# Layer norm with tokens on partitions by eight turns, masks in 64x32 blocks, rope tables renewed one by one

## The reference

```
for i in range(6):
    x = attn_layer(shift_tokens(x), Wqkv[i], q_scale[i], k_scale[i], Wo[i]) + x
    x = ffn_layer(shift_tokens(x), ln_g[i], ln_b[i], W1[i], b1[i], W2[i], b2[i]) + x

def ffn_layer(x, g, bln, W1, b1, W2, b2):
    mu = x.mean(-1, keepdims=True)
    var = ((x - mu) ** 2).mean(-1, keepdims=True)
    xn = (x - mu) / jnp.sqrt(var + 1e-05) * g + bln
    a, gate = jnp.split(xn @ W1 + b1, 2, -1)
    return a * gelu(gate) @ W2 + b2
```

## Time and profile before

| | |
|---|---|
| median of 3 runs | 3816.27 us (3815.24 to 3817.18) |
| the profiled execution | 3817.41 us |
| its span, first to last instruction | 3815.5 us |
| mean granted PE clock | 0.981 of full |
| instructions | 146379 |
| span up to the layers | some 675 us |
| the layers | some 3125 us for 384 slots |

### The profile page before, as it was taken

One profiled execution on the slowest core, in us unless ns is written; L12 is line 12 of the kernel. 1 busy time (PEld: TensorE's weight loads), 2 busy tenths in 40 slices (PEclk: granted clock), 3 DMA queues, 4 the chain that ended last, 5 costly groups with the idle time before them and its releaser, 6 DMA issues.

```text
span 3815.5 us, 146379 instructions
## 1 busy us (share of the span) xinstructions
PE 3549.1 (93%) x60112; PEld 2231.2 (58%) x60128; DVE 3112.5 (82%) x4377; ACT 2650.5 (69%) x4972; POOL 2420.8 (63%) x2197
## 2 busy tenths in 40 slices
PE   5667676899999999999999999999999999999997
PEld 2222222466666666666666666666666666666664
DVE  4899998888888888888878888878888788888884
ACT  3545454677777777777777777777777777777775
POOL 0356555776666666666666666666666666666661
PEclk9889899999999999999999999999999999999999
DMA  3000000010111111111111111111111111111101
GB/s 78 0 0 0 0 0 0 26 37 28 33 35 48 37 33 32 32 48 37 37 33 32 43 43 35 30 32 32 48 41 34 32 32 48 37 37 29 33 28 38
DMA packets 64418, 120.05 MB, mean 31 GB/s; under 512 B 18196, under 2 KB 35986, under 8 KB 63634
## 3 DMA queue, kind: packets, MB, share of 16 engines
q1 hardware_dynamic: 63762, 110.70, 10.0%
HBM read 20.50 MB, written 2.10 MB: 6 GB/s over the span
## 4 chain that ended last, share of the span: by engine, by line
PE 79%; issue 2%; DVE 2%; ACT 1%; POOL 0%; DMA 0%; ACTq 0%; POOLq 0%; DVEq 0%; SPq 0%
PE qk L1130 17%; PE trb L1002 10%; PE ob L1188 10%; PE vob L1196 8%; PE vob L1136 8%; PE sc L1164 7%; PE sc L1215 6%; PE ob L1002 4%; PE sc L1222 3%; PE sc L1158 2%; PE vob L1238 1%; PE vob L1250 1%; DVE arena L889 0%; DVE ssq L895 0%; DVE arena L890 0%
## 5 line engine op out<-in xcount | busy, mean ns | idle before, releaser
L507 POOL TENSOR_TENSOR arena<-arena,rnorm 128x512 f32<-128x512 f32 x768 | 785.2, 1044 | 930.0 <-ACT rnorm L626 929.5
L500 POOL TENSOR_TENSOR arena<-arena 128x512 f32<-128x512 f32 x768 | 962.8, 1275 | 35.9 <-DVE arena L890 35.9
L633 ACT ACTIVATE arena<-trb 128x512 f32<-128x512 f32 x768 | 462.6, 602 | 441.6 <-PE trb L1002 441.6
L1130 PE MATMUL qk<-wqkv,xs 128*128 128x512 f32 x1536 | 729.4, 597 | 16.3 <-issue 9.2
L889 DVE TENSOR_TENSOR arena<-qk,tab_q 128x512 f32<-128x512 f32 x384 | 263.3, 686 | 455.0 <-ACT arena L619 447.6
L483 POOL TENSOR_TENSOR arena<-arena 128x512 f32<-128x512 f32 x256 | 300.0, 1182 | 346.4 <-DVE arena L859 333.8
L1002 PE MATMUL trb<-ident,arena 128*128 128x128 f32 x3072 | 482.3, 280 | 9.8 <-ACT arena L633 7.3
L1130 PEld LDWEIGHTS qk<-wqkv,xs 128*128 128x128 f32 x1536 | 292.7, 191 | 309.1 <-issue 291.7
L895 DVE TENSOR_REDUCE ssq<-arena 128x16 f32<-128x1024 f32 x384 | 463.7, 1207 | 0.0
L619 ACT ACTIVATE arena<-qk 128x512 f32<-128x512 f32 x768 | 426.8, 588 | 45.0 <-PE qk L1130 28.1
L1002 PEld LDWEIGHTS trb<-ident,arena 128*128 128x128 f32 x3072 | 346.7, 141 | 140.1 <-issue 88.3
(11 more groups left out here) (139 smaller groups left out, 5879.6 us busy)
## 6 DMA issues: line engine op xcount, KB each, us to landing
arena<-arena SPq DMA_DIRECT2D x192, 384.0 KB, 3.2
arena<-arena SPq DMA_DIRECT2D x192, 64.0 KB, 3.0
wqkv<-in_L_ffn_Wqkv SPq DMA_DIRECT2D x18, 512.0 KB, 4.6
wo<-in_L_ffn_Wo SPq DMA_DIRECT2D x6, 512.0 KB, 4.0
arena<-in_L_attn_x SPq DMA_DIRECT2D x8, 256.0 KB, 2.9
out<-arena SPq DMA_DIRECT2D x8, 256.0 KB, 2.2
w<-in_L_ffn_W SPq DMA_DIRECT2D x6, 341.0 KB, 2.9
arena<-in_sel SPq DMA_DIRECT2D x1, 1024.0 KB, 5.0
```

Of the source, the lines that this page charges most:

```text
L500: nc.gpsimd.tensor_tensor(ts[c * 2 + j][:, heads], tu[:, 0, heads], tu[:, 1, heads], ALU.add).then_inc(summed[0], 1)
L507: nc.gpsimd.tensor_tensor(part, part, rnorm[j][:, 8 * h:8 * h + 8].unsqueeze(2).to_broadcast([P, 8, HEAD]), ALU.mult) \
L633: A((qT, kT)[j][u][:, 4 * h:4 * h + 4, at_col:at_col + P], TRB.rearrange("p (a t) -> p a t", a=4), ACT.Copy) \
L1130: MM(QK[:, 512 * h:512 * h + 512], lhsT=xs[u][:, c * P:(c + 1) * P], rhs=wqkv[:, col:col + 512], start=True, stop=True) \
```

## The change

The norm of a group takes another way. In slot 19 (`LAG_TOKENS`) PE turns `xs2` in four blocks of 128x128, so that tokens lie on partitions (`VOB`). DVE sums each token's 128 features along the free axis (four sums for each partition) and subtracts the mean (`centre`). In slot 20 (`LAG_SQUARES`) ACT squares, and DVE sums again at the slot's end. In slot 21 (`LAG_BACK`) ACT takes logarithm and exponential of four numbers for each partition, DVE multiplies behind its rope, PE turns the result back in four blocks into the second half of `SC`, behind the down product, and ACT applies gain and offset on the way to `xnT`. The scores of the next slot wait for that. `v_unit` of slot 19 waits for the subtraction (`n_xc`). The copy of the layer's parameters moves from slot 22 to slot 21 behind the addition of the last down product.

The mask of a step is written by eight products instead of two, each on a 64x32 tile, with a semaphore increment in PE's queue ahead of them. The constant is changed so that rows 64 to 127 repeat rows 0 to 63. The rope tables of the next layer are multiplied one in each slot, in the slot behind a table's last use.

The diff, without the declarations of the new semaphores and of four small buffers `nsum`, `nvar`, `nlog`, `nrstd` (128x4):

```diff
@@ -39,7 +39,7 @@
 LAG_SCORES, LAG_SUM, LAG_PTURN, LAG_VALUES, LAG_OUT, LAG_ADD = 6, 7, 8, 9, 10, 11
-LAG_STAGE, LAG_MEAN, LAG_VAR, LAG_NORMED = 17, 19, 21, 22
+LAG_STAGE, LAG_TOKENS, LAG_SQUARES, LAG_BACK = 17, 19, 20, 21
 LAG_UP, LAG_DOWN = (23, 25, 27), 29
...
@@ -681,6 +695,12 @@
                     squares(*unit)
+                at_ = group_at(l, k, LAG_BACK)
+                if at_:
+                    act_e.wait_ge(n_var[0], at_[1] + 1)
+                    A(nlog[:], nvar[:], ACT.Ln, scale=1.0 / DIM, bias=eps[:, 0:1]).then_inc(n_log[0], 1)
+                    act_e.wait_ge(n_log[0], at_[1] + 1)
+                    A(nrstd[:], nlog[:], ACT.Exp, scale=-0.5).then_inc(n_rstd[0], 1)
                 up0, up1 = group_at(l, k, LAG_UP[0]), group_at(l, k, LAG_UP[1])
...
@@ -692,17 +712,17 @@
                     turned(*at_, 0)
-                at_ = group_at(l, k, LAG_MEAN)
-                if at_:
-                    item(act_e, ln_xc, at_[1] + 2 * GROUPS)
-                    A(sq2[0], xc[0], ACT.Square).then_inc(ln_sq[0], 1)
-                at_ = group_at(l, k, LAG_VAR)
-                if at_:
-                    item(act_e, ln_var, at_[1] + 2 * GROUPS)
-                    item(act_e, ln_out, at_[1] + (2 * GROUPS - 1))
-                    A(rstd[0], bank[2][:], ACT.Ln, bias=eps[:, 0:1]).then_inc(ln_log[0], 1)
-                    item(act_e, ln_log, at_[1] + 2 * GROUPS)
-                    A(rstd[0], rstd[0], ACT.Exp, scale=-0.5).then_inc(ln_rstd[0], 1)
+                at_ = group_at(l, k, LAG_SQUARES)
+                if at_:
+                    act_e.wait_ge(n_xc[0], at_[1] + 1)
+                    A(sq2[0], xc[0], ACT.Square).then_inc(n_sq[0], 1)
+                at_ = group_at(l, k, LAG_BACK)
+                if at_:
+                    if at_[0] == 0:
+                        item(act_e, lpar_done, l + (k - LAG_BACK) // LAYER)
+                    item(act_e, n_back, at_[1])
+                    A(xnT[:, at_[0] * GROUP:at_[0] * GROUP + GROUP], SC[:, 512:1024], ACT.Identity, scale=lpar[:, 0:1], bias=lpar[:, 1:2]) \
+                        .then_inc(n_out[0], 1)
                 at_ = step_at(l, k, LAG_VALUES)
...
@@ -871,12 +891,10 @@
 
-            def layer_tables(l, layer):
-
-                for c in range(CHUNKS):
-                    for tab, base, sc in ((tab_q, base_q, scale_q), (tab_k, base_k, scale_k)):
-                        V.tensor_tensor(tab[:, c], base[:, c], sc[:, ds(layer, 1), :].to_broadcast([P, 2, HEAD]), ALU.mult) \
-                            .then_inc(tabs_done[0], 1)
+            def layer_table(layer, c, j):
+
+                tab, base, sc = (tab_q, tab_k)[j], (base_q, base_k)[j], (scale_q, scale_k)[j]
+                V.tensor_tensor(tab[:, c], base[:, c], sc[:, ds(layer, 1), :].to_broadcast([P, 2, HEAD]), ALU.mult).then_inc(tabs_done[0], 1)
 
...
@@ -931,6 +949,17 @@
 
+            def centre(group, n):
+
+                dve.wait_ge(n_turned[0], n + 1)
+                tokens = VOB[:, :].rearrange("p (c f) -> p c f", f=DIM)
+                V.tensor_reduce(nsum[:], tokens, op=ALU.add, axis=AX.X).then_inc(n_sum[0], 1)
+                slot(dve, n_back, n)
+                dve.wait_ge(n_sum[0], n + 1)
+                V.scalar_tensor_tensor(out=xc[0].rearrange("p (c f) -> p c f", f=DIM),
+                                       in0=nsum[:, :].unsqueeze(2).to_broadcast([P, GROUP // P, DIM]), scalar=-1.0 / DIM,
+                                       in1=tokens, op0=ALU.mult, op1=ALU.add).then_inc(n_xc[0], 1)
+
             def layer_slot(l, k):
...
@@ -939,21 +968,21 @@
                 unit = unit_at(l, k, 0)
-                if unit and k % LAYER == 0:
-                    layer = l + k // LAYER
-                    if k:
-                        item(dve, roped, unit[0] * 2 + -1)
-                    layer_tables(l, layer)
-                    item(dve, tabs_done, layer * (2 * CHUNKS) + (2 * CHUNKS - 1))
+                if unit and k % LAYER < UNITS:
+                    dve.wait_ge(tabs_done[0], (l + k // LAYER) * UNITS + k % LAYER + 1)
                 if unit:
                     rope(*unit)
+                at_ = group_at(l, k, LAG_BACK)
+                if at_:
+                    dve.wait_ge(n_rstd[0], at_[1] + 1)
+                    tokens = xc[0].rearrange("p (c f) -> p c f", f=DIM)
+                    V.tensor_tensor(tokens, tokens, nrstd[:, :].unsqueeze(2).to_broadcast([P, GROUP // P, DIM]), ALU.mult).then_inc(n_scaled[0], 1)
                 at_ = step_at(l, k, LAG_SCORES)
...
                     maxima(*at_)
-                at_ = group_at(l, k, LAG_MEAN)
-                if at_:
-                    item(dve, ln_mean, at_[1] + 2 * GROUPS)
-                    V.tensor_tensor(xc[0], xs2.rearrange("p s t -> p (s t)"), bank[2][:], ALU.subtract).then_inc(ln_xc[0], 1)
+                at_ = group_at(l, k, LAG_TOKENS)
+                if at_:
+                    centre(*at_)
                 at_ = group_at(l, k, LAG_UP[1])
...
@@ -964,22 +993,29 @@
                     add_y(*at_)
+                at_ = group_at(l, k, LAG_BACK)
+                if at_ and at_[0] == 0:
+                    layer = l + (k - LAG_BACK) // LAYER
+                    if group_at(l, k, LAG_DOWN):
+                        item(dve, x_next, layer * GROUPS + -1)
+                    V.tensor_copy(lpar[:], lpar_all[:, ds(layer, 1), :].rearrange("p o n -> p (o n)")).then_inc(lpar_done[0], 1)
+                    item(dve, lpar_done, layer)
                 if unit:
                     square_sums(*unit)
-                at_ = group_at(l, k, LAG_NORMED)
-                if at_:
-                    if at_[0] == 0:
-                        layer = l + (k - LAG_NORMED) // LAYER
-                        V.tensor_copy(lpar[:], lpar_all[:, ds(layer, 1), :].rearrange("p o n -> p (o n)")).then_inc(lpar_done[0], 1)
-                        item(dve, lpar_done, layer)
-                    item(dve, ln_rstd, at_[1] + 2 * GROUPS)
-                    V.scalar_tensor_tensor(out=xc[0], in0=xc[0], scalar=lpar[:, 0:1], in1=rstd[0], op0=ALU.mult, op1=ALU.mult) \
-                        .then_inc(ln_aff[0], 1)
-                    item(dve, ln_aff, at_[1])
-                    V.tensor_scalar(xnT[:, at_[0] * GROUP:at_[0] * GROUP + GROUP], xc[0], lpar[:, 1:2], None, ALU.add).then_inc(ln_out[0], 1)
+                ahead = unit_at(l, k, 1)
+                if ahead and not isinstance(l, int) and LAYER - UNITS <= (k - 1) % LAYER:
+                    item(dve, roped, ahead[0] * 2 + 1)
+                    layer_table(l + 1, ahead[3], ahead[4])
+                at_ = group_at(l, k, LAG_SQUARES)
+                if at_:
+                    dve.wait_ge(n_sq[0], at_[1] + 1)
+                    V.tensor_reduce(nvar[:], sq2[0].rearrange("p (c f) -> p c f", f=DIM), op=ALU.add, axis=AX.X).then_inc(n_var[0], 1)
 
...
             dve.wait_ge(cleared[0], 2)
+            for c in range(CHUNKS):
+                for j in range(2):
+                    layer_table(0, c, j)
             item(dve, ln_out, 2 * GROUPS - 1)
...
@@ -994,7 +1030,7 @@
         def _(pe):
-            give_credits(pe, [x_turned, y_step, mo_done, vproj_done, tr_done, s_done, pt_done, pv_done, wo_done, y_done, f_turned])
+            give_credits(pe, [x_turned, y_step, mo_done, vproj_done, tr_done, s_done, pt_done, pv_done, wo_done, y_done, n_back, f_turned])
             MM = nc.tensor.matmul
...
@@ -1141,7 +1177,7 @@
 
-            def scores(s, B, u, j, n, up0, up1, up2, down):
+            def scores(s, B, u, j, n, up0, up1, up2, down, back):
 
...
@@ -1154,9 +1190,14 @@
                     item(pe, x_next, down[1])
-                for h in range(2):
-                    MM(SC[:, 512 * h:512 * h + 512], lhsT=ident16[:], rhs=mask[:, :].unsqueeze(1).to_broadcast([P, STEP_PAIRS, 2 * SPAN]),
-                       start=True, stop=True)
+                if back:
+                    pe.wait_ge(n_out[0], back[1] + 1)
+                pe.sem_inc(s_open[0], 1)
+                for g in range(4):
+                    for h in range(2):
+                        d, pick = slice(64 * h, 64 * h + 64), 64 * h + (WINDOW if g else 0)
+                        MM(SC[32 * g:32 * g + 32, 512 * h:512 * h + 512], lhsT=ident16[d, pick:pick + WINDOW],
+                           rhs=mask[d, :].unsqueeze(1).to_broadcast([64, STEP_PAIRS, 2 * SPAN]), start=True, stop=True, skip_group_check=True)
                 for a in range(STEP_PAIRS):
...
@@ -1229,13 +1270,7 @@
                 out_before = step_at(l, k - 1, LAG_OUT)
-                mean = group_at(l, k, LAG_MEAN)
-                var = group_at(l, k, LAG_VAR)
-                if var:
-                    pe.wait_ge(ln_sq[0], var[1] + (1 + 2 * GROUPS))
-                    if out_before:
-                        item(pe, x_added, out_before[0])
-                    MM(VOB[:, :], lhsT=meanw[:], rhs=sq2[0], start=True, stop=True).then_inc(ln_var[0], 1)
```

(35 more changed lines are left out.)

18 lines of the change are left out of this document (16 added, 2 removed).

## The result

The changed kernel took 4060.35 us (median of 4 runs, 4051.55 to 4073.37) against 3816.72 for the kernel before on the same chip: ratio 1.0639, 95% interval 1.0615 to 1.0664, 244 us slower. The forecast was 3891 us in a range of 3850 to 3940. Its sign was right, its size was not: the loss was three times the one it named. The profiled execution of after took 4055.68 us, its span 4053.8.

What follows compares the result with a forecast made beforehand. TensorE (93% busy) bounds the kernel; later transposes (+2.13 us) less three mask gains of 0.18 cost 1.6 us a group, 74 over 46 groups, with the tail +75 on 3816.3: 3891 us, range 3850 to 3940.

Steps and rivals of the forecast that it cites:

- What bounds the kernel, and where it bites: PE bounds the layers; in slot 21 it waits about 2.3 us for VectorE's multiply, some 46 times.
- PE's own work, -0.85 a group: Mean and variance products go (1.72 us a group), eight 128x128 turns come (0.87) in slots 19 and 21.
- The mask, m=0.18: Eight tile products shorten mask start to scores start by m, 0.18 us a step, bounds 0.07 to 0.21.
- all at once: Case where the eight mask tiles overlap fully: 0.215 us, mask to scores 0.31, against 0.36 at 4.8 at once.
- The estimate of 0.41: Skill-based estimate for the eight mask tiles: 0.41 us against the old pair's 0.43, sum 2.1 us a group.
- VectorE's chain: Reduce and subtraction in slot 19 add 0.82 us, the reduce in slot 20 0.65, delaying slot 21's rope and multiply.
- The multiply, 0.67: VectorE's multiply behind the rope of slot 21, priced as a quarter of a rope, ends 0.67 us later.
- later by DVE's delay: GpSimd starts its sums and scales later by VectorE's delay; the transposes needing them come two slots on.
- a rival at 0.11: Clock falls behind each stall: up to 1.7 us more a group, 3969; in half the groups 3930; chance 0.11.
- Stall at v_unit, 0.8: In slot 19 PE waits 0.8 us for the new subtraction, lying under the wait in slot 21.
- Tables and ACT at nothing: Table products spread over four slots cost nothing; ScalarE's moved square and last scaling hide behind its waits for PE.
- my first rival: The wait in slot 21 is covered and PE's savings come through: 1.57 us a group, 3741; chance 0.10.

Runs made afterwards that it cites:

- kernel with the adds held back: Changed kernel with GpSimd's adds of the unit of slot 21 waiting for VectorE's multiply: 3994.51 us, ratio 1.0451.
- the added products: Changed kernel, GpSimd's adds held until after the multiply, plus two unread 512-column products on PE before its wait for the multiply: 3912.15 us, ratio 1.0243.
- kernel with the turns late: Changed kernel with the four turns back and ScalarE's last scaling moved behind v_unit of slot 21: 3824.15 us, ratio 1.0007.
- two lines of order: Changed kernel with VectorE's multiply put ahead of its rope in slot 21, nothing else: 3834.83 us, ratio 1.0047.

## Why the prediction was wrong, point by point

Two terms of the sum failed. The slow clock behind the gap stood in it at nothing and is worth 82 to 117 us; the multiply stood in it at 0.67 us, took 1.71 beside GpSimd, and that is worth some 40 us. Either failure alone leaves the range: 3994.51 us was measured without the contention, 3953.92 nearly without the slow clock. With neither it was 3912.15, inside the range. The wait itself was found.

- **What bounds the kernel, and where it bites: right.** PE ran on without idle time, so a wait in its queue shows in full. The place, the releaser and the count are as forecast (slot 21, multiply, 46).
- **PE's own work, -0.85 a group: right.** 13.7 less 7.0 us a turn at full clock is 0.84.
- **The mask, m=0.18: right,** 0.20, and 28 us by itself. The value of "all at once" (0.215) was the one met. The mask alone gave 28 us and not 192 times 0.20. The estimate of 0.41 for the eight tiles, by the page of the Trainium skill that the prediction names, is what the busy column shows (0.41 for x8), but not what the next product waits for: that is 0.23. I set this duration against 0.43, a distance of starts; by the busy column the old pair has 0.59.
- **VectorE's chain: right to 0.1 us an operation.** The rows of after, of slots 19 and 20:

```profile
1983.85 0.68 DVE L956 TENSOR_REDUCE nsum<-vob 128x4 f32<-128x512 f32 x1
...
1984.63 0.69 DVE L959 SCALAR_TENSOR_TENSOR arena<-nsum,vob 128x512 f32<-128x512 f32 x1
...
1995.18 0.68 DVE L1012 TENSOR_REDUCE nvar<-arena 128x4 f32<-128x512 f32 x1
...
1995.77 0.41 DVE L937 TENSOR_TENSOR xT<-vob,xT 128x256 f32<-128x256 f32 x1
```

  Reduce to subtraction 0.78 (forecast 0.75), the subtraction 0.69 (0.66), the new reduce 0.59 to the next start (0.65). With the multiply at its 0.68 the gap is 2.06 (kernel with the adds held back), forecast 2.3. The kernel that has this chain and neither contention nor a slow clock is 93 us over before, forecast 75; its idle time put down to issue, which I had at nothing, and some 6 us of the added products are in the 93.
- **The multiply, 0.67: this term failed first in time.** I priced it as "a quarter of a rope" with the duration of L956. Both read PSUM. I did not look at what GpSimd does when it starts. In before, GpSimd's pair of adds starts 0.49 us behind the end of the rope (100.97):

```profile
2101.46 2.52 POOL L500 TENSOR_TENSOR arena<-arena 128x512 f32<-128x512 f32 x2
```

  GpSimd is released, through ScalarE, by the sum of squares of slot 20. The new reduce stands behind that sum on VectorE, so the rope is later against GpSimd by its 0.59, and the add now comes 0.1 ahead of the multiply. I had GpSimd "later by DVE's delay". The Trainium skill ("SBUF — State Buffer", section "SBUF: two separate sides") says that a VectorE instruction with two SBUF inputs and a GpSimd instruction that reads SBUF contend for one shared port pair, and that whichever starts first has it for its whole instruction. The trace agrees (the two adds at 1999.84 one by one, min, median and max in ns):

```profile
L514 POOL TENSOR_TENSOR arena<-arena x2: 1262/1494/1726, 1999.8 to 2001.1; 128x512 f32<-128x512 f32 x2
```

  The first add, 1.26 us, ends at 2001.10, the multiply needs 0.55 after that and ends at 2001.65, and the second add takes 1.73 where two usual ones take 2.51. It cost some 40 us by itself, and it made the gap 3.09.
- **The clock: the largest miss, at nothing in the sum and a rival at 0.11.** I had two gaps in the earlier trace rows, took 2.25 as the safe side and set 2.3 next to it. The runs say that gaps near 2.06 and 2.25 both go either way, and that most of them lose. The trace of before could not warn of that: it has four gaps of 2.18 to 2.48 us at the turn of the loop, and the granted clock stayed at 1.00 behind each. In the kernels with the mask alone and the tables alone it fell behind two of the same four. Its price was low too: 1.7 from a window of 5 us in the earlier trace rows, where 7.5 us are slow and cost 3.1. With 3.1 in every group it would be 143 us. Measured are 106 with the gap of 3.09 and 82 with the gap of 2.06 (3994.5 less 3912.2). So without any contention the time would still have been 3994.51, far over my upper end.
- **Stall at v_unit, 0.8, "costs nothing of its own": right here** (0.63 on average, under the gap of slot 21). It is what shows once that gap is gone: 30.3 us in all in the kernel with the turns late.
- **Tables and ACT at nothing: right** for the tables (3821.53); for ACT no run isolates it, and the only wait for its new scaling in PE's list is 0.9 us, once.
- **Range.** Its upper end, 3940, had no contention in it and the clock in half of the groups at half its price.

The rest of the distance to 3741, the forecast of my first rival, was not found: each version without the gap pays some 30 us for the subtraction or for what is moved, and has more idle time put down to issue. The best kernel measured is the mask alone, 3792.66 us.

## What to carry to other kernels

When an operation is put on an engine, look at which memories it reads and what the neighbour that shares a port is doing at that moment; a duration from an operation that reads PSUM is no price for one that reads SBUF twice. A wait that opens a gap of 2 us or more in TensorE's queue must be costed with the work behind it at the lower clock, even when the trace at hand has such gaps at full clock: here four of four kept it before the change, and most lost it after. Work put ahead of the wait, or the waiting work put later, costs less than the gap. Change the order first: two lines of order were worth 226 us here, three times the 75 us that the change saves in TensorE's own work by the forecast.
